# Expert rows found by one-hot products and fetched, and expert weights moved by transfers, in an attention and mixture-of-experts layer

## The chip, the cores and the metric

The kernel runs on one core of a Trainium2 chip. Times are device microseconds of one execution. The engines are TensorE (PE; PEld is its weight load), VectorE (DVE), ScalarE (ACT), GpSimd (POOL) and SyncE (SP), which here only issues transfers. Sixteen DMA engines carry all transfers, whichever queue issues them.

## What is computed

`x` is 16 x 256 x 128. After a layer norm without weights, two branches read the same `xn`:

```python
xn = _layernorm(x, axis=-1)
# attention: 16 heads of 8, causal, with a rising position bias; q, k, v have a low-rank addition
s = s + alibi[None] + mask
p = jax.nn.softmax(s, axis=-1)
o = einsum(p, v) ; s = o @ Wp.T
# experts: each token goes to the one expert of 8 with the largest logit
indices = jnp.argmax(softmax(xn @ Wr + br), axis=-1)
for i in range(num_experts):
    mask = (indices == i)[..., None]
    h = jax.nn.relu((xn * mask) @ W1[i] + b1[i])
    out = out + (h @ W2[i] + b2[i])
return x + s * silu(out)
```

The 4,096 tokens have one expert each (128 to 512 hidden to 128). For the seven other experts a token's row of `xn` is zero, so they add a constant row, worked out once.

## The kernel before, in words

**The loop.** After a prologue, every engine runs the same two loops: 16 iterations `i` (one batch of 256 tokens each), each of six groups `g` (`NG`). A group holds two units of scores (the last one): PE computes the scores of batch `i` (L1142, mask L1150) and, for the row maxima, those of batch `i + 2` (L1122, mask L1130). DVE takes the row maxima (L807), ACT the exponentials (L698), PE multiplies them with the values (L1193). Between them, at fixed groups, lie the rest of a batch's work: the turned maxima (L1204, L618), which SP writes into the stack of queries (L383); the output copied out of its bank by ACT (`keep_o`, L688), turned (L1213), divided (L921, L926), turned back (L1220) and projected (L1227); and the projection of batch `i + 4` (L1070), cut into three bf16 parts (L596, L781, L602, L498) that SP stores into the stack (L345, L351, L378). Eight stores of batch `i + 3` are issued at the start of iteration `i`, two more and the maxima in group 3. PE, DVE and ACT share banks of PSUM in a fixed turn (four for DVE, three for ACT); `VEC` and `ACTS` number the uses.

**The experts.** Logits are taken in iteration 0, the best expert, the counts per tile and each token's slot (`slot_of`, L876) at the end of iteration 0 and the start of iteration 1. Slots are sorted by expert and padded to tiles of 128, at most 39 (`SLOT_TILES`). A table of slots in DRAM (`sorted_rows`) is cleared in iteration 0 (L390, five transfers), and from iteration 1 to 6 POOL scatters one tile of normalised rows per group, with the token's number beside each row (L505, 32 of them). At the start of iteration 7, when all have landed, SP loads four tiles of sorted rows at a time (L412); POOL keeps the numbers (L512).

**A tile** `t` then is: PE turns the rows (four tiles at once, `turn_rows`, L1235) and ACT copies them (L675); ACT reads the expert's number and copies its 578 KB of weights from `w_all` into one of three slots (`copy_weights`, L682), one tile ahead; PE `hidden` (L1243), DVE relu with the bias (L933), PE `output` (L1251) one group later, DVE adds the constant row (L939), POOL scatters the result to the tokens' places (L518). One tile stands in each group, from group 43 (7, 1) on. `TILES_AT`, `TURN_AT` and the other tables map a place `(i, g)` to it. The eight expert weights are loaded in iterations 1 to 4 (L402), the constant rows computed in iteration 5 (L1263, 64 records).

**The end.** From group 84 on SP loads the experts' results (L421), ACT takes the tanh (L670), DVE multiplies (L954, L960), DVE or POOL adds x, SP stores. The last batch is finished behind the loop.

## Time and profile before

| | us |
|---|---|
| median of 3 runs | 356.69 (356.25 to 358.17) |
| the profiled execution | 357.79 |
| its span, first to last instruction | 356.0 |
| PE busy | 303.9 (85%) |
| DVE, ACT, POOL busy | 215.9, 208.0, 115.3 |
| mean granted clock of PE | 0.922 of full speed |

Busy time of an engine is the union of its instructions; matmuls are pipelined, so a busy PE need not be at its peak. Iterations are told apart in the trace by L688, ACT's copy of the output, once per iteration from iteration 1 on: 74.1, 90.1, 105.4, 118.9, 132.1, 155.3, 167.0, 198.2, 220.8, 242.9, 265.5, 287.5, 309.0, 326.3, 338.1 and 347.7 us.

### The profile page before, as it was taken

The page shows a single profiled execution, that of the slowest core. Times are in us where ns is not written, and L with a number is a line of the kernel's source. Part 1 is how long each engine was busy: PE and PEld are TensorE (multiplying, and loading weights), DVE is VectorE, ACT ScalarE, POOL GpSimd, SP SyncE. Part 2 cuts the span into 40 slices and gives each one's busy share as a digit, 9 for nine tenths or more (in the row PEclk, how much of TensorE's full clock was granted, in tenths as well). Part 3 has the DMA queues.
Part 4 walks back from the last instruction along what each step waited for, and adds up shares of the span by engine and source line. Part 5 has one row for each costly group of instructions (what it writes and reads, how often), then busy time and mean ns, then how long its engine had stood idle before and what let it go on. Part 6 is the DMA issues. An engine that isn't in the chain of part 4 may idle for free.

```text
span 356.0 us, 12916 instructions
## 1 busy us (share of the span) xinstructions
PE 303.9 (85%) x5244; PEld 234.3 (66%) x5244; DVE 215.9 (61%) x501; ACT 208.0 (58%) x380; POOL 115.3 (32%) x143
## 2 busy tenths in 40 slices
PE   6866697988778879986299999999999999999773
PEld 2445585755555557654188888888888888887542
DVE  3747893475856751674065756757567575664495
ACT  2242235256657661567177777777777776766881
POOL 5532191006355550441022242422424222222150
PEclk9966589579999999899589999999999999999997
DMA  7995340235365662142402422225222241010753
GB/s 191 225 194 126 103 160 28 113 79 176 106 203 151 179 206 54 45 111 51 125 18 60 127 70 72 59 58 133 71 67 61 63 126 42 17 31 19 215 148 115
DMA packets 47946, 37.36 MB, mean 105 GB/s; under 512 B 5016, under 2 KB 44824, under 8 KB 47760
## 3 DMA queue, kind: packets, MB, share of 16 engines
q1 hardware_dynamic: 43856, 29.73, 30.9%
q0 software_dynamic: 2272, 4.92, 4.2%
q10 hardware_dynamic: 1760, 1.89, 2.6%
q8 instruction: 42, 0.69, 0.9%
q14 instruction: 16, 0.13, 0.1%
HBM read 13.46 MB, written 9.96 MB: 66 GB/s over the span
## 4 chain that ended last, share of the span: by engine, by line
PE 70%; DVE 8%; issue 7%; DMA 6%; ACT 5%; SPq 2%; ACTq 1%; DVEq 0%
PE bank L1243 11%; PE bank L1193 10%; PE bank L1142 10%; PE bank L1251 9%; PE bank L1070 4%; PE bank L1077 3%; PE bank L1150 3%; PE bank L1227 3%; PE bank L1122 2%; PE bank L1086 2%; PE bank L1213 2%; PE bank L1263 2%; PE bank L1235 2%; DMA dense<-w_dense 2%; DVE row_max L807 1%
## 5 line engine op out<-in xcount | busy, mean ns | idle before, releaser
L807 DVE TENSOR_REDUCE row_max<-bank 128x2 f32<-128x512 f32 (+3 forms) x176 | 107.1, 638 | 53.1 <-PE bank L1130 44.0
L698 ACT ACTIVATE probs<-bank 128x512 f32<-128x512 f32 (+1 forms) x176 | 91.6, 559 | 48.5 <-PE bank L1150 41.1
L1142 PE MATMUL bank<-qk_stack 64*64 64x64 bf16 (+3 forms) x1024 | 64.7, 241 | 10.4 <-issue 3.6
L1122 PE MATMUL bank<-qk_stack 64*64 64x64 bf16 (+3 forms) x1024 | 68.6, 252 | 5.0 <-DVE row_max L807 1.8
L518 POOL DMA_INDIRECT expert_rows<-y_slot,token_of x39 | 37.7, 967 | 95.0 <-DVE y_slot L939 95.0
L1142 PEld LDWEIGHTS bank<-qk_stack 64*64 64x64 bf16 x1024 | 36.8, 110 | 28.5 <-issue 16.0
L1193 PE MATMUL bank<-probs,v_diag 128*32 128x64 f32 (+3 forms) x1024 | 50.2, 313 | 3.6 <-issue 3.3
L505 POOL DMA_INDIRECT sorted_rows<-rows_all,slot_of x32 | 31.0, 970 | 59.7 <-PE bank L1150 55.9
L682 ACT ACTIVATE w_slots<-w_all 128x1156 f32 x39 | 45.5, 1167 | 4.0 <-issue 2.7
L1130 PE MATMUL bank<-cb 64*64 64x128 bf16 (+2 forms) x352 | 46.7, 259 | 0.1
L933 DVE TENSOR_TENSOR hT<-bank,w_slots 128x512 f32<-128x512 f32 x39 | 26.9, 690 | 30.9 <-PE bank L1243 30.9
L1243 PE MATMUL bank<-xsT_slot,w_slots 128*128 128x128 f32 x312 | 44.4, 283 | 1.3 <-issue 0.8
L1150 PE MATMUL bank<-cb 64*64 64x128 bf16 (+2 forms) x352 | 45.3, 248 | 0.0
L1122 PEld LDWEIGHTS bank<-qk_stack 64*64 64x64 bf16 x1024 | 38.1, 115 | 7.7 <-DVE row_max L807 2.9
L1243 PEld LDWEIGHTS bank<-xsT_slot,w_slots 128*128 128x128 f32 x312 | 38.7, 192 | 4.3 <-issue 2.9
L1251 PE MATMUL bank<-w_slots,hT 128*128 128x128 f32 x312 | 41.2, 275 | 0.0
L1251 PEld LDWEIGHTS bank<-w_slots,hT 128*128 128x128 f32 x312 | 38.0, 192 | 0.0
L1193 PEld LDWEIGHTS bank<-probs,v_diag 128*32 128x32 f32 x1024 | 26.8, 112 | 16.7 <-issue 5.9
L498 POOL TENSOR_TENSOR parts<-rem,parts 128x512 bf16<-128x512 f32 x16 | 18.4, 1153 | 31.9 <-ACT parts L602 31.3
L1130 PEld LDWEIGHTS bank<-cb 64*64 64x64 bf16 x352 | 21.6, 117 | 0.7 <-issue 0.3
L1070 PE MATMUL bank<-xnT_all,w_eff 128*128 128x256 f32 x64 | 19.4, 435 | 2.6 <-ACT xnT_all L590 2.0
L1150 PEld LDWEIGHTS bank<-cb 64*64 64x64 bf16 x352 | 20.9, 111 | 0.7 <-issue 0.6
(122 smaller groups left out, 369.6 us busy)
## 6 DMA issues: line engine op xcount, KB each, us to landing
qk_stack<-parts SPq DMA_DIRECT2D x120, 64.0 KB
qk_stack<-parts SPq DMA_DIRECT2D x32, 128.0 KB
w_all<-w_experts SPq DMA_DIRECT2D x8, 512.0 KB
sorted_rows<-w_all SPq DMA_DIRECT2D x5, 576.0 KB, 3.9
xs_slot<-sorted_rows SPq DMA_DIRECT2D x9, 288.0 KB
rows_all<-expert_rows SPq DMA_DIRECT2D x8, 256.0 KB, 4.2
out<-rows_all SPq DMA_DIRECT2D x7, 256.0 KB, 2.3
x_all<-x SPq DMA_DIRECT2D x3, 512.0 KB, 15.0
```

The lines of the kernel that those rows point to most:

```text
L518: pool.indirect_dma_start(y_dram[:, :], bass.IndirectOffsetOnAxis(token_of[:, t:t + 1], axis=0), y_slot[:, t % 3, :], None).then_inc(S[f"y ...
L682: act.activation(w_slot[t % 3], w_all[:, bass.ds(e, 1), :].rearrange("p o f -> p (o f)"), ACT.Copy).then_inc(S["w_done"], 1)
L698: act.activation(probs[:, m % PROBS, 0:w], bank[:, 0:w], ACT.Exp).then_inc(emptied, 1)
L807: dve.tensor_reduce(row_max[b % 2][:, n, pairs[0]:pairs[-1] + 1], bank[:, 0:ln_u * len(pairs)].rearrange("p (c k) -> p c k", k=ln_u), AX.X ...
L1070: last = pe.matmul(bank[:, n * T:(n + 1) * T], w_eff[:, n, :], xnT_all[:, b, :], start=(n == 0), stop=True, skip_group_check=True)
L1122: pe.matmul(bank[to, c * ln_u:(c + 1) * ln_u], q[rows, p, n * BLK:(n + 1) * BLK], k[rows, p, 0:(n + 1) * BLK], start=(c == 0), stop=False, ...
L1130: last = pe.matmul(bank[to, 0:ln_u * len(pairs)].rearrange("p (c k) -> p c k", k=ln_u)[:, :, n * BLK:], ident_b[rows, rows], mask_qk[rows] ...
L1142: pe.matmul(bank[rows, c * ln_u:(c + 1) * ln_u], k[rows, p, kb * BLK:(kb + 1) * BLK], q[rows, p, kb * BLK:], start=(c == 0), stop=False, s ...
L1150: last = pe.matmul(bank[rows, 0:ln_u * len(pairs)].rearrange("p (c k) -> p c k", k=ln_u)[:, :, 0:BLK], ident_b[rows, rows], mask_kq[rows]. ...
L1193: last = pe.matmul(pv_bank[32 * j:32 * j + 32, half * T + kb * BLK:(half + 1) * T], v_diag[b % 2][:, kb, p, :], probs[:, (b * NU + w) % PR ...
L1243: last = pe.matmul(bank[:, c * P:(c + 1) * P], w_slot[t % 3][:, c * P:(c + 1) * P], xsT_slot[:, t // 4 % 2, t % 4, :], start=(c == 0), sto ...
L1251: last = pe.matmul(bank[:, 0:D], hT[:, t % 2, c, :], w_slot[t % 3][:, W2 + c * D:W2 + (c + 1) * D], start=(c == 0), stop=(c == NC_H - 1))
```

## The change

- **Whose row a slot holds** is found by products. DVE splits a token's slot into tile and row (`r32[:, 4]`, `r32[:, 5]`), DVE and POOL make one-hot arrays of both in iteration 1, and PE multiplies them (`slot_tokens`, 32 products at (1, 5)); DVE keeps the token numbers (`from_row`, `token_of`).
- **Rows.** SP stores the normalised rows in order (`keep_rows`, four transfers of 512 KB); POOL fetches 128 rows per tile with an indirect transfer (`fetch_rows`), eight tiles ahead. Clearing, scattering and the loads of sorted rows go.
- **Weights.** `copy_weights` issues a transfer from ACT's queue into the slot, SBUF to SBUF, with a semaphore per slot, in place of an activation.
- **Places.** Tiles start at group 17 (2, 5) in place of 43, four per iteration (groups 5, 0, 2, 3) in place of six. The constant rows move from iteration 5 to 2, the expert loads to iterations 0 and 1, the bias columns to (0, 2), the last part from group 84 to 77.

```diff
-FIRST_SCATTER = NG + 2
-FIRST_TILE = FIRST_SCATTER + NT + 3
-TURNS = list(range(FIRST_TILE, FIRST_TILE + SLOT_TILES))
+ROWS_TURN = 2 * NG + 4
+TILE_OFFSETS = (1, 2, 4, 5)
+TURNS = [ROWS_TURN + t // 4 * NG + TILE_OFFSETS[t % 4] for t in range(SLOT_TILES + 1)]
...
 TILES_AT = {place: (t,) for t, place in enumerate(PLACES)}
-SCATTER_AT = {divmod(FIRST_SCATTER + n, NG): n for n in range(NT)}
 QUADS = (SLOT_TILES + 3) // 4
-ROWS_PLACE = divmod(FIRST_TILE - 1, NG)
-TURN_AT = {PLACES[max(4 * q - 2, 0)]: q for q in range(1, QUADS)} | {ROWS_PLACE: 0}
...
-EXPERT_AT = {(1 + e // 2, 4 + e % 2): e for e in range(E)}
+ROWS_PLACE = divmod(ROWS_TURN, NG)
+TURN_AT = {PLACES[4 * q - 2]: q for q in range(1, QUADS)} | {ROWS_PLACE: 0}
+FETCH_AT = {divmod(ROWS_TURN - 3 + n, NG): (2 * n, 2 * n + 1) for n in range(4)}
+FETCH_AT |= {PLACES[t - 8]: (t,) for t in range(8, SLOT_TILES)}
+EXPERT_AT = {(0, g): g for g in range(NG)} | {(1, 1): 6, (1, 2): 7}
+KEEP_ROWS_AT = {(0, 3): 0, (0, 4): 1, (0, 5): 2, (1, 4): 3}
 K_ON_ACT = 2
-CROW_AT = (5, 1)
-CROW_SPREAD_AT = (5, 2)
+CROW_AT = (2, 2)
+CROW_SPREAD_AT = (2, 3)
...
+HOT_AT = {(1, 1): "high", (1, 2): 0, (1, 3): 1, (1, 4): "ids"}
+HOT_VEC, HOT_POOL = (0, 1), (2, 3)
+IDS_AT = (1, 5)
 
 
 CHUNK = 4
 CHUNKS = NT // CHUNK
-FIRST_LOAD = TURNS[-1] + 3
+FIRST_LOAD = TURNS[-1] + 2
...
-            def clear_rows(c):
+            def keep_rows(c):
 
                 if c == 0:
-                    sp.wait_ge(S["zero_rows_src"], 1)
-                rows = ROWS_PER_P // ZERO_CHUNKS
-                sp.dma_start(xs_dram.rearrange("(p n r) d -> p n (r d)", p=P, n=ZERO_CHUNKS)[:, c],
-                             clear_src[:, c * rows:(c + 1) * rows].rearrange("p r d -> p (r d)")).then_inc(S["zeros_out"], 16)
+                    sp.wait_ge(S["xn_vec"], len(NORM_VEC))
+                    sp.wait_ge(S["xn_act"], len(NORM_ACT))
+                sp.wait_ge(S["xn_pool"], len([n for n in NORM_POOL if n < 8 * (c + 1)]))
+                sp.dma_start(xn_tiles[:, 8 * c:8 * (c + 1), :], xn_all[:, 8 * c:8 * (c + 1), :]).then_inc(S["rows_kept"], 16)
...
-            def load_rows(q):
-                tiles = min(4, SLOT_TILES - 4 * q)
-                if q == 0:
-                    sp.wait_ge(S["scattered"], 16 * NT)
-                if q >= 2:
-                    k, use = ACTS["rows", q - 2]
-                    sp.wait_ge(act_full[k], use + 1)
-                    sp.wait_ge(S["tokens_kept"], q - 1)
-                sp.dma_start(xs_slot[:, q % 2, 0:tiles, :],
-                             xs_dram[4 * q * P:(4 * q + tiles) * P].rearrange("(j p) d -> p j d", p=P)).then_inc(S[f"xs_in{q % 2}"], 16)
...
-            def scatter(n):
-
-                pool.indirect_dma_start(xs_dram[:, :], bass.IndirectOffsetOnAxis(slot_of[:, n:n + 1], axis=0),
-                                        rows_all[:, n, :], None).then_inc(S["scattered"], 16)
-
-            def keep_tokens(q):
-
-                pool.wait_ge(S[f"xs_in{q % 2}"], 16 * (q // 2 + 1))
-                tiles = min(4, SLOT_TILES - 4 * q)
-                pool.tensor_copy(token_of[:, 4 * q:4 * q + tiles], xs_slot[:, q % 2, 0:tiles, ROW_TOKEN].bitcast(U32)).then_inc(S["tokens_kept"], 1)
+            def row_onehot(c):
+
+                for n in range(8 * c, 8 * (c + 1)):
+                    pool.tensor_scalar(row_hot[:, n, :], iota_row, r32[:, 5, n:n + 1], None, ALU.is_equal).then_inc(S["row_hot_pool"], 1)
+
+            def fetch_rows(t):
+
+                q = t // 4
+                if t == 0:
+                    pool.wait_ge(S["rows_done"], 1)
+                    pool.wait_ge(S["rows_kept"], 16 * 4)
+                if q >= 2:
+                    wait_act_full(pool, "rows", q - 2)
+                pool.indirect_dma_start(xs_slot[:, q % 2, t % 4, :], None, xn_dram[:, :],
+                                        bass.IndirectOffsetOnAxis(from_row[:, t:t + 1], axis=0)).then_inc(S[f"xs_in{t % 8}"], 16)
...
                 e = act.value_load(tile_expert[0:1, t:t + 1], min_val=0, max_val=E - 1)
                 if t >= 3:
                     wait_vec_emptied(act, "y", t - 3)
-                act.activation(w_slot[t % 3], w_all[:, bass.ds(e, 1), :].rearrange("p o f -> p (o f)"), ACT.Copy).then_inc(S["w_done"], 1)
+                act.dma_start(w_slot[t % 3], w_all[:, bass.ds(e, 1), :].rearrange("p o f -> p (o f)")).then_inc(S[f"w_in{t % 3}"], 16)
...
-                dve.tensor_copy(slot_of[:, :], r32[:, 3, :]).then_inc(S["slots_done"], 1)
+                then(dve.tensor_copy(r32i[:, 0, :], r32[:, 3, :]))
+                then(dve.tensor_scalar(r32i[:, 1, :], r32i[:, 0, :], P.bit_length() - 1, None, ALU.arith_shift_right))
+                then(dve.tensor_copy(r32[:, 4, :], r32i[:, 1, :]))
+                dve.scalar_tensor_tensor(r32[:, 5, :], r32[:, 4, :], -float(P), r32[:, 3, :], ALU.mult, ALU.add).then_inc(S["slots_done"], 1)
+
+            def tile_onehot():
+
+                hot = [P, NT, SLOT_ROWS]
+                then(dve.tensor_tensor(tile_hot[:, :, 0, :], iota_slot.unsqueeze(1).to_broadcast(hot),
+                                       r32[:, 4, :].unsqueeze(2).to_broadcast(hot), ALU.is_equal))
+
+            def tile_numbers():
+
+                then(dve.tensor_tensor(tile_hot[:, :, 1, :], tile_hot[:, :, 0, :], tile_ids.unsqueeze(2).to_broadcast([P, NT, SLOT_ROWS]), ALU.mult))
+                dve.tensor_scalar(tile_hot[:, :, 0, :], tile_hot[:, :, 0, :], place1, None, ALU.mult).then_inc(S["tile_hot_done"], 1)
+
+            def row_onehot(c):
+
+                dve.wait_ge(S["slots_done"], 1)
+                tiles = slice(8 * c, 8 * (c + 1))
+                dve.tensor_tensor(row_hot[:, tiles, :], iota_row.unsqueeze(1).to_broadcast([P, 8, P]),
+                                  r32[:, 5, tiles].unsqueeze(2).to_broadcast([P, 8, P]), ALU.is_equal).then_inc(S["row_hot_vec"], 1)
+
+            def keep_ids():
+
+                bank, emptied = wait_vec_full(dve, "ids")
+                then(dve.tensor_copy(r40[:, 0, :], bank[:, 0:SLOT_ROWS]))
+                dve.scalar_tensor_tensor(r40[:, 1, :], bank[:, SLOT_ROWS:2 * SLOT_ROWS], float(P), r40[:, 0, :], ALU.mult, ALU.add).then_inc(emptied, 1)
+                wait_vec_emptied(dve, "ids")
+                dve.tensor_scalar(from_row[:, :], r40[:, 1, :], -1.0, 0.0, ALU.add, ALU.max).then_inc(S["rows_done"], 1)
+                then(dve.scalar_tensor_tensor(r40[:, 0, :], r40[:, 1, :], 0.0, spare_ids, ALU.is_equal, ALU.mult))
+                dve.scalar_tensor_tensor(token_of[:, :], r40[:, 1, :], -1.0, r40[:, 0, :], ALU.add, ALU.add).then_inc(S["tokens_done"], 1)
...
-                    if (i, g) == (2, 1):
+                    if (i, g) == (0, 2):
+                        bias_columns()
+                    if (i, g) in HOT_AT:
+                        if HOT_AT[i, g] == "high":
+                            tile_onehot()
+                        elif HOT_AT[i, g] == "ids":
+                            tile_numbers()
+                        else:
+                            row_onehot(HOT_AT[i, g])
+                    if (i, g) == IDS_AT:
+                        keep_ids()
+                    if (i, g) == (2, 0):
...
+            def slot_tokens():
+
+
+                pe.wait_ge(S["tile_hot_done"], 1)
+                bank, full = begin_vec("ids")
+                for n in range(NT):
+                    if n // 8 in HOT_VEC:
+                        pe.wait_ge(S["row_hot_vec"], n // 8 + 1)
+                    else:
+                        pe.wait_ge(S["row_hot_pool"], n + 1 - 8 * len(HOT_VEC))
+                    last = pe.matmul(bank[:, 0:2 * SLOT_ROWS], row_hot[:, n, :], tile_hot[:, n].rearrange("p c h -> p (c h)"),
+                                     start=(n == 0), stop=(n == NT - 1))
+                last.then_inc(full, 1)
...
-                pe.wait_ge(S[f"xs_in{q % 2}"], 16 * (q // 2 + 1))
                 bank, full = begin_act("rows", q)
                 for j in range(min(4, SLOT_TILES - 4 * q)):
+                    pe.wait_ge(S[f"xs_in{(4 * q + j) % 8}"], 16 * (q // 2 + 1))
                     last = pe.transpose(bank[:, j * P:(j + 1) * P], xs_slot[:, q % 2, j, 0:D], ident_f)
                 last.then_inc(full, 1)
 
             def hidden(t):
-                pe.wait_ge(S["w_done"], t + 1)
+                pe.wait_ge(S[f"w_in{t % 3}"], 16 * (t // 3 + 1))
```

The order of PE in an iteration with tiles, before (scores and masks left out; L1193 products with the values, L1235 turn of rows, L1243 and L1251 hidden and output, L1213, L1220, L1227 the attention output, L1204 the maxima):

```order
L1235 MATMUL bank<-cf,xs_slot 128x128 x4
L1243 MATMUL bank<-xsT_slot,w_slots 128x128 x4
L1251 MATMUL bank<-w_slots,hT 128x128 x4
...
L1193 MATMUL bank<-probs,v_diag 32x256 x8
L1204 MATMUL bank<-cb,nmax 32x64 x8
L1243 MATMUL bank<-xsT_slot,w_slots 128x128 x4
L1251 MATMUL bank<-w_slots,hT 128x128 x4
...
L1220 MATMUL bank<-cf,o_tok 128x128 x2
L1077 MATMUL bank<-w_v,xnT_all 64x64 x8
L1243 MATMUL bank<-xsT_slot,w_slots 128x128 x4
```

And after, from group 1 to group 3 of an iteration (line numbers of the changed kernel: L1271 turn of rows, L1279 hidden, L1287 output):

```order
L1249 MATMUL bank<-cf,oT 128x128 x4
L1092 MATMUL bank<-xnT_all,w_eff 128x256 x2
...
L1229 MATMUL bank<-probs,v_diag 32x256 x8
L1240 MATMUL bank<-cb,nmax 32x64 x8
L1271 MATMUL bank<-cf,xs_slot 128x128 x4
L1279 MATMUL bank<-xsT_slot,w_slots 128x128 x4
L1287 MATMUL bank<-w_slots,hT 128x128 x4
...
L1256 MATMUL bank<-cf,o_tok 128x128 x2
L1099 MATMUL bank<-w_v,xnT_all 64x64 x8
L1279 MATMUL bank<-xsT_slot,w_slots 128x128 x4
```

Group 1 has no tile now; the turn of rows stands in group 2, straight ahead of a hidden product, and groups 2 and 3 keep one tile each.

ACT in groups 2 and 3, before (L698 exponentials, L602 second part, L618 maxima, L682 the copy of weights):

```order
192 L602 ACTIVATE parts<-rem 128x512 [waits q2_out3,vec_empty2]
193 L618 ACTIVATE nmaxT<-bank 64x256 [waits act_full2,max_in0]
194 L679 TENSOR_LOAD tile_expert
195 L679 ISA x2
196 L682 ISA
197 L682 ACTIVATE w_slots<-w_all 128x1156
198 L698 ACTIVATE probs<-bank 128x384 [waits act_full0,pv_ps]
```

and after (L679 exponentials, L583, L599 and L656 as L602, L618 and L675 before):

```order
120 L583 ACTIVATE parts<-rem 128x512 [waits q2_out3,vec_empty2]
121 L599 ACTIVATE nmaxT<-bank 64x256 [waits act_full2,max_in0]
122 L656 ACTIVATE xsT_slot<-bank 128x512 [waits act_full0]
123 L660 TENSOR_LOAD tile_expert
124 L660 ISA x2
125 L663 ISA [waits vec_empty2]
126 L663 DMA w_slots<-w_all 128x1156
127 L679 ACTIVATE probs<-bank 128x384 [waits act_full1,pv_ps]
```

The transfer is issued where the copy stood, one tile ahead of its use, and in group 2 the copy of turned rows stands ahead of it.

DVE in iteration 1 after the change, groups 1 to 5 (L789 row maxima, L866, L871, L872 the tile one-hots, L878 the row one-hots, L884 on the token numbers); before, only the row maxima stood there:

```order
L866 TENSOR_TENSOR w_slots<-cf,r 128x32x40
L763 TENSOR_TENSOR rem<-bank,parts 128x512
L789 TENSOR_REDUCE row_max<-bank 128x2 x2
L878 TENSOR_TENSOR w_slots<-cf,r 128x1024
L789 TENSOR_REDUCE row_max<-bank 128x2 x2
L878 TENSOR_TENSOR w_slots<-cf,r 128x1024
L789 TENSOR_REDUCE row_max<-bank 128x4 x2
L871 TENSOR_TENSOR w_slots<-w_slots,cf 128x32x40
L872 TENSOR_SCALAR w_slots<-w_slots,cf 128x32x40
L789 TENSOR_REDUCE row_max<-bank 128x8
L884 COPY r<-bank 128x40
```

Five large passes now stand between the row maxima for which PE's banks wait.

## Rows read from the trace of the kernel before

**Rows 1.** The page, busy time: us, share of the span, instructions.
```profile
PE 303.9 (85%) x5244; PEld 234.3 (66%) x5244; DVE 215.9 (61%) x501; ACT 208.0 (58%) x380; POOL 115.3 (32%) x143
```
**Rows 2.** Busy time by stretch, core 0: iterations 1, 2, 5, 6, 7, 9, 14, 15, tail.
```profile
core 0: us, PE busy (x) PEld busy (x) DVE busy (x) ACT busy (x) POOL busy (x), PEclk, DMA share, GB/s
74.10:90.10 16.00, 12.46 (x292) 8.52 (x294) 10.82 (x30) 9.40 (x20) 6.19 (x6) 0.98 0.47 140
90.10:105.40 15.30, 11.90 (x277) 7.75 (x271) 10.58 (x28) 8.94 (x19) 6.93 (x7) 1.00 0.51 156
...
132.10:155.30 23.20, 21.52 (x364) 15.11 (x357) 10.85 (x22) 9.20 (x19) 6.92 (x7) 0.93 0.22 59
155.30:167.00 11.70, 10.06 (x262) 6.94 (x253) 8.01 (x17) 8.88 (x20) 4.05 (x4) 1.00 0.32 81
167.00:198.20 31.20, 22.31 (x357) 18.54 (x358) 13.48 (x30) 16.95 (x28) 5.44 (x7) 0.84 0.27 73
...
220.80:242.90 22.10, 21.91 (x377) 18.83 (x376) 14.15 (x30) 16.47 (x26) 7.13 (x8) 1.00 0.25 68
...
326.30:338.10 11.80, 9.54 (x195) 6.58 (x190) 4.74 (x9) 9.57 (x23) 1.28 (x1) 1.00 0.58 163
338.10:347.70 9.60, 7.39 (x140) 4.47 (x136) 9.50 (x13) 7.50 (x18) 4.60 (x3) 1.00 0.56 158
347.70:356.00 8.30, 2.32 (x10) 1.55 (x10) 4.42 (x10) 0.98 (x2) 0.00 (x0) 0.72 0.35 101
```
**Rows 3.** Timeline of SP at 172, the chain of waits there, and the list of waits.
```profile
172.47 1.14 SPq L412 DMA_DIRECT2D xs_slot<-sorted_rows  x2
```
```profile
172.47 3.15 DMA xs_slot<-sorted_rows
```
```profile
PE bank L1235 <- DMA xs_slot<-sorted_rows: 8.8, 1, 8.8
```
**Rows 4.** Timeline of PE, iterations 8 and 9: start us, us, engine, line.
```profile
205.76 1.16 PE L1243 MATMUL bank<-xsT_slot,w_slots 128*128 128x128 f32 x8
206.76 1.06 PE L1251 MATMUL bank<-w_slots,hT 128*128 128x128 f32 x8
207.75 0.27 PE L1142 MATMUL bank<-qk_stack 64*64 64x192 bf16 x2
...
209.41 1.16 PE L1243 MATMUL bank<-xsT_slot,w_slots 128*128 128x128 f32 x8
...
216.49 1.06 PE L1243 MATMUL bank<-xsT_slot,w_slots 128*128 128x128 f32 x8
```
```profile
220.48 1.14 PE L1243 MATMUL bank<-xsT_slot,w_slots 128*128 128x128 f32 x8 [0.43 <-issue]
```
**Rows 5.** The chain of waits, the constant rows.
```profile
134.30 7.08 PE bank L1263 x64
```
**Rows 6.** Groups by shape: count, busy us, mean ns, idle before.
```profile
L682 ACT ACTIVATE w_slots<-w_all 128x1156 f32 x39 | 45.5, 1167 | 4.0 <-issue 2.7
L501 POOL TENSOR_SCALAR rows_all<-x_all,rstd,nmr 128x128 f32<-128x128 f32 x27 | 11.7, 450 | 12.0 <-DVE nmr L770 11.9
L807 DVE TENSOR_REDUCE row_max<-bank 128x2 f32<-128x512 f32 x64 | 42.3, 686 | 22.4 <-PE bank L1130 15.4 <-issue 2.6 <-remote 2.3
L960 DVE TENSOR_TENSOR rows_all<-rows_all,xnT_all 128x512 f32<-128x512 f32 x7 | 6.9, 992 | 0.0
L954 DVE SCALAR_TENSOR_TENSOR rows_all<-w_slots,rows_all 128x512 f32<-128x512 f32 x8 | 6.7, 836 | 5.8 <-ACT w_slots L670 5.8
L852 DVE TENSOR_TENSOR xs_slot<-xs_slot,cf 128x256 f32<-128x256 f32 x1 | 0.4, 426 | 0.0
```
**Rows 7.** L390, stores of 576 KB: issue to landing; one microsecond while three are under way.
```profile
DMA to landing us min/median/max: 2.9/3.9/6.8
```
```profile
44.00:45.00 1.00, 1.00 (x14) 0.48 (x11) 1.00 (x3) 0.00 (x0) 1.00 (x3) 0.50 1.04 424
```
**Rows 8.** Timeline of ACT's queue: a store issued beside an activation.
```profile
19.46 0.54 ACTq L351 DMA_DIRECT2D qk_stack<-parts  x1
```

101 lines of the change are left out of this document (44 added, 57 removed).

## The prediction

> **What bounds the kernel now.** The busy line of the page comes first: TensorE 85%, the others 32 to 61% [rows 1]. That is an average, so the second view is busy time by stretch, one stretch per iteration of the loop over the 16 batches (from one copy of the attention output out of the banks to the next) [rows 2]. Read PE's busy time against the stretch. With six expert tiles in an iteration (220.8 to 242.9) PE is busy 21.91 of 22.10 us: it is the bound, ACT and DVE have 5.6 and 8 us to spare. Without tiles (155.3 to 167.0) the same attention takes 11.7 us, PE busy 10.06: about 1.4 us goes into hand-overs between engines. Iterations 1 and 2 take 16.0 and 15.3. Two stretches stand out: 23.2 us, which holds the constant rows (7.08 us of PE in the chain of waits [rows 5]), and 31.2 us, the first with tiles. The third view, waits and the chain around 172, says why: the first load of sorted rows leaves SP at 172.47, behind eight stores of projections, lands after 3.15 us, and PE has waited 8.8 us [rows 3]; it then runs part of the stretch at the lower clock (granted 0.84 on average, 1.00 in its neighbours) [rows 2].
>
> So there are four places with slack: that start, the tile-free iterations where PE idles, the last two iterations (9.54 of 11.8 and 7.39 of 9.6 us busy), and the tail. PE's own work must be done whatever its order.
>
> **The change, part by part.** Times are of the profiled execution (span 356.0, its own time 357.79); I move only the difference onto the median 356.69. Everything before 74.1 I leave as it is: expert loads take the place of the zero stores in the same queue, and three copies of normalised rows (512 KB each) are added there behind a queue whose next stores go out at 71. From 74.1 to the end is 281.9 us before. The same part after, iteration by iteration:
>
> 1. Iterations 3 to 11, four tiles each. A tile costs PE 1.99 us here (205.76 to 207.75, hidden and output products) and somewhat under where it doesn't follow a small product; I take 1.9 [rows 4]. Attention, six tiles and one turn of rows are 22.1; less 2 x 1.9 is 18.3. Two of six groups now have no tile to cover hand-overs; a tile-free iteration loses 1.4 over all six, of which I put 0.3 here. 18.6 x 9 = 167.4.
> 2. Iteration 12: two hidden and three output products left, 22.1 - 3.5 x 1.9 = 15.4.
> 3. Iteration 1. VectorE gets two compares of 1,024 elements per partition, three passes of 1,280 and about nine small ones. 256 elements take 0.426 and 512 take 0.686 us [rows 6], so 1,024 cost 1.2, 1,280 cost 1.5, a small one 0.2 (estimates): 2.4 + 4.4 + 1.6 = 8.4 us. VectorE is busy 10.82 of 16.0, so 5.2 hide and 3.2 do not. PE then runs 32 products; nothing like them is in the trace, the 64 of the constant rows take 0.11 each, so at most 3.5 us, at least nothing exposed, and I take 1.3 beyond what VectorE's backlog covers. GpSimd makes 16 one-hots at 0.45 = 7.2 us [rows 6] where scatters were; it finishes before PE's last group. 16.0 + 4.5 = 20.5.
> 4. Iteration 2 takes in the constant rows: 23.2 - 11.7 = 11.5 with its hand-overs, 10.5 where the stretch is looser anyway; one turn of rows and one hidden product, 1.5; the scatters and expert loads that made it longer than 11.7 are gone, -2.0. 15.3 + 10.5 + 1.5 - 2.0 = 25.3.
> 5. Iterations 13 to 15 and the tail. The gates now start two groups into iteration 13, where VectorE still has its 11 row maxima (8 us busy in a tile-free iteration); four products at 0.84 and three at 0.99 [rows 6] bring it to 14.3, so 14.5. Iteration 14 goes from 11.8 to 10.3 (PE 9.54 plus hand-overs; nothing waits for the last scatter any more), 15 from 9.6 to 8.5 (PE 7.39; VectorE, busy 9.50 of 9.6 before, has only the last gates), the tail from 8.3 to 7.5, since the last division no longer queues behind gates. 40.8.
>
> Sum 167.4 + 15.4 + 20.5 + 25.3 + 40.8 = 269.4 against 281.9: **-12.5 us** if every weight transfer is hidden. The start of the tiles is in it: the rows are fetched by GpSimd two to three groups ahead and no longer queue on SP.
>
> 6. The weights. ACT's copy is 1.17 us, 39 times [rows 6], but ACT doesn't bound, so taking it away is worth nothing by itself; an issue takes ACT's queue 0.54 us beside the activation that runs [rows 8]. What counts is the time from issue to landing, since tile t+1's transfer is issued in tile t's group and PE waits for it. The nearest row is a store of 576 KB with 128 runs of 4.6 KB, against 578 KB here in the same runs: 2.9 us at least, 3.9 median (several of them queued behind one another), 6.8 at most, at 424 GB/s in the full microsecond [rows 7]. The time that PE gives it: hidden product to hidden product in neighbouring groups is 3.65 us (205.76 to 209.41) and 3.99 (216.49 to 220.48) [rows 4]; the issue comes about 0.5 after the first of them (the read of the expert's number, and in every other case the copy of turned rows ahead of it). That leaves 3.15 and 3.5. Nineteen of the 38 gaps are of that kind, the others span two groups and have 2 us more. Alone the transfer fits by 0.2 to 0.6 us. But 39 x 578 KB is 23 MB, four transfers an iteration at 1.5 us of all 16 engines = 6 us, beside the 0.25 of the engines' time in use now in an iteration with tiles [rows 2], which comes in bursts. I take 0.3 us of wait on each of the nineteen: **+6 us**. Ends: 0 (2.9 always) and 19 x 1.2 = +23 (4.4 us, the median plus half a microsecond).
>
> The Trainium skill ("DMA: Bandwidth & Descriptors", section "Anatomy of one DMA") gives a fixed cost of about 2.0 us plus bytes over 436 GB/s for a transfer: by our arithmetic 3.4 us here, 0.5 over the 2.9 of the row. By it alone the 3.15 us gaps would wait 0.2 each and the longer ones not at all, some 2 us in all; the row's minimum would give none.
>
> -12.5 + 6 = -6.5: 356.7 - 6.5 = **350.2 us**.
>
> **Rivals.** (A) *The transfers land late*, and that is the one that ends slower. Mechanism: ACT's transfers meet the eight stores of projections and the row maxima's transfer; at 4.4 us to landing the nineteen waits cost 1.2 each and the sum is -12.5 + 23 = +10.5, 367 us. It decides from 0.66 us per wait on (12.5 / 19), that is from landings of some 4.0 us, hardly over the median of the row. For it: the second issue of ACT slips when ACT is behind; the transfer reads and writes SBUF, which the row doesn't. Against: DMA is in use for a quarter of an iteration with tiles now [rows 2], and SP's stores go out 0.6 us apart, so a large transfer gets most of the engines. The skill (same page, "Issuing engines are not separate DMA queues") says that transfers interleave on the same engines whoever issues them; the row on which this bears is the most loaded one, 6.8 us.
>
> (B) *All hidden*: -12.5, 344 us. For it, the minimum of 2.9 and the two-group gaps; a wait also lets ACT and VectorE catch up for the tile-free group behind it.
>
> (C) *The order costs more than it gives*: iteration 1 bound by VectorE at 24 instead of 20.5 and a low clock after PE's idling, iterations 3 to 11 at 19.0 instead of 18.6: +3.5 +3.6 = 357, no change.
>
> That the change doesn't do what it says would be that ACT's issues hold its exponentials up as long as the copies did; at 0.54 against 1.17 and with ACT at three quarters busy this changes nothing.
>
> **How the numbers follow.** Forecast (347 to 354.5): 0.38. B (under 347): 0.24. C (355 to 358.5): 0.12. A (over 358.5): 0.26. The range 340 to 366 leaves out the ends of A and B, about 0.15 to 0.2. Faster by over 0.5% (about what a measurement of this kernel can tell from no change), under 354.9: 0.62; within 0.5%: 0.12; slower: 0.26.
>
> **What would show it.** Right: no wait of 8 us before the first turn of rows; iterations 3 to 11 at 18.6 to 19.2 us, PE busy over 95%; landings of the weights at 3.0 to 3.7 us and PE's waits on them under 0.6 us each, nineteen or fewer; iteration 1 at 20 to 21 us with VectorE over 90% busy; iteration 14 near 10. Wrong: iterations at 20 us or more with the hidden product waiting on the transfer (A), or waits elsewhere in iterations 1, 2 and 13 (C). If the load on the DMA engines delays the projections' stores, the first scores of an iteration would wait for them; that would be a mechanism that I have priced at nothing, because the last of them and the row maxima go out in group 3, some 8 us before PE needs them.

## Result and profile after

| | median, us | range | runs |
|---|---|---|---|
| before | 357.43 | 356.25 to 359.91 | 4 |
| changed | 378.51 | 377.01 to 379.74 | 4 |

The ratio is 1.0578, with a 95% interval of 1.0507 to 1.065: 5 to 6.5% slower. The forecast was 350.2, with a range that ended at 366. Some executions of a kernel come out more than 1.5% above its fastest; the ratios, and the medians marked with a star below, leave them out.

The page of the changed kernel, its head and the groups that answer to [rows 1] and [rows 6]; of a group: busy time, mean duration of one, and the idle time of the engine just before them with what ended it.

```profile
span 375.1 us, 12978 instructions
PE 305.3 (81%) x5276; PEld 236.1 (63%) x5276; DVE 220.0 (59%) x514; ACT 162.4 (43%) x341; POOL 128.8 (34%) x152
...
q10 hardware_dynamic: 7376, 24.97, 18.7%
...
DMA w_slots<-w_all 19%; PE bank L1279 8%; PE bank L1287 6%; PE bank L1178 5%; PE bank L1229 4%; PE bank L1186 3%; ACT probs L679 3%; PE bank L1249 2%; PE bank L1092 2%; PE bank L1299 2%; PE bank L1263 1%; DVE rem L763 1%; DMA xn_all<-expert
...
L1279 PE MATMUL bank<-xsT_slot,w_slots 128*128 128x128 f32 x312 | 49.2, 300 | 33.4 <-DMA w_slots<-w_all 25.2
```

TensorE is still the busiest engine, but at 81% instead of 85%, and the chain that ended last now holds a transfer for a fifth of the span: `w_slots<-w_all`, the experts' weights. It is the new entry, and PE waited 25.2 us for it ahead of the hidden products (L1279). The weights are 23 of the 25 MB on q10, ACT's queue.

The same stretches as in [rows 2], one per iteration (PE, PEld, DVE, ACT, POOL busy, then the granted clock of PE, the DMA engines' share and GB/s): iterations 1 to 5, then 10 to 15 and the tail.

```profile
71.40:93.20 21.80, 14.59 (x315) 10.24 (x317) 18.18 (x44) 9.10 (x19) 15.07 (x17) 0.89 0.47 132
93.20:121.20 28.00, 23.09 (x359) 16.87 (x356) 12.15 (x26) 9.52 (x20) 10.87 (x11) 0.88 0.31 94
121.20:143.00 21.80, 19.20 (x350) 15.70 (x349) 12.42 (x26) 9.76 (x21) 9.04 (x9) 1.00 0.50 164
143.00:165.30 22.30, 18.94 (x345) 15.26 (x344) 12.42 (x26) 9.36 (x21) 9.03 (x9) 1.00 0.51 169
165.30:189.10 23.80, 19.12 (x345) 15.36 (x344) 12.47 (x26) 9.38 (x21) 9.03 (x9) 1.00 0.52 168
...
281.00:300.20 19.20, 17.54 (x339) 14.32 (x338) 12.54 (x26) 9.56 (x21) 6.08 (x6) 1.00 0.56 179
300.20:322.50 22.30, 19.61 (x341) 16.40 (x341) 12.42 (x26) 9.34 (x20) 5.03 (x5) 0.92 0.48 159
322.50:337.50 15.00, 14.36 (x318) 11.32 (x322) 9.55 (x20) 7.95 (x18) 2.88 (x3) 1.00 0.37 108
337.50:349.00 11.50, 9.90 (x270) 6.72 (x262) 11.16 (x23) 9.88 (x24) 2.55 (x2) 1.00 0.71 205
349.00:360.10 11.10, 8.87 (x184) 6.18 (x182) 10.00 (x18) 9.10 (x22) 2.59 (x2) 1.00 0.43 123
360.10:368.10 8.00, 7.49 (x146) 4.68 (x142) 0.78 (x2) 5.65 (x13) 0.00 (x0) 1.00 0.14 37
368.10:375.10 7.00, 1.80 (x10) 1.14 (x10) 2.39 (x6) 0.98 (x2) 0.00 (x0) 0.86 0.13 37
```

Iterations 3 to 11 run from 121.2 to 322.5 and take 201.3 us, 22.4 each, where 18.6 was forecast. PE is busy 17.5 to 20.2 of each, so it no longer fills them. The first load of rows, for which PE waited 8.8 us in [rows 3], has no such wait any more: that part of the change works.

What PE waited for in those nine iterations (us in total, times, longest):

```profile
PE bank L1279 <- DMA w_slots<-w_all: 19.6, 16, 3.4
PE bank L1279 <- issue: 8.0, 10, 2.5
```

Sixteen waits at 19.6 / 16 = 1.2 us. Eleven of them, 14.6 us, stand on gaps of one group between two tiles, and five, 5.0 us, on gaps over two groups, to which the prediction gave no wait. Besides, "issue": PE stood still and the profile shows nothing that it waited for. Three of these ten (1.6, 1.9 and 2.5 us, just ahead of a hidden product) may well be weights too; the other seven are 0.2 to 0.5 us long, and such stops come back below.

A wait on a gap of one group, ACT's queue and then PE; the hidden product of the tile before starts at 286.65:

```profile
287.49 0.51 ACTq L663 DMA_DIRECT2D w_slots<-w_all  x1
...
291.06 1.16 PE L1279 MATMUL bank<-xsT_slot,w_slots 128*128 128x128 f32 x8 [0.78 <-DMA w_slots<-w_all]
```

The issue comes 0.84 us after the product before it and the weights land 3.6 us later: 4.4 together, where PE gets there in 3.6.

A wait on a gap over two groups. The hidden product of the tile before starts at 175.36:

```profile
176.94 0.49 ACT L679 ACTIVATE probs<-bank 128x384 f32<-128x384 f32 x1 [2.41 <-remote]
177.32 0.38 ACT L640 ACTIVATE o2T<-bank 128x256 f32<-128x256 f32 x1
177.59 0.37 ACT L590 ACTIVATE v_diag<-bank 64x256 f32<-64x256 f32 x1
177.87 0.50 ACTq L663 DMA_DIRECT2D w_slots<-w_all  x1
...
183.19 1.05 PE L1279 MATMUL bank<-xsT_slot,w_slots 128*128 128x128 f32 x7 [2.26 <-DMA w_slots<-w_all]
```

The transfer is issued 2.5 us after the hidden product before it, behind an exponential and two copies in ACT's queue ("remote": released by a queue that the profile doesn't name), and lands 5.3 us later. The prediction had 0.5 and 2.9 to 3.9.

### The profile page after: what moved, and what is told of

It is laid out like the page before. It is cut to its first block, busy times and chain, and to the rows that moved or that the text cites. A ratio compares the mean times of both kernels' runs of the same rounds, so it can differ in the third digit from the quotient of the medians.

```text
span 375.1 us, 12978 instructions
## 1 busy us (share of the span) xinstructions
PE 305.3 (81%) x5276; PEld 236.1 (63%) x5276; DVE 220.0 (59%) x514; ACT 162.4 (43%) x341; POOL 128.8 (34%) x152
## 3 DMA queue, kind: packets, MB, share of 16 engines
q10 hardware_dynamic: 7376, 24.97, 18.7%
## 4 chain that ended last, share of the span: by engine, by line
PE 37%; DMA 21%; ACT 6%; issue 5%; DVE 4%; another core or an unknown queue 2%; ACTq 1%; POOL 0%; DVEq 0%; SPq 0%
DMA w_slots<-w_all 19%; PE bank L1279 8%; PE bank L1287 6%; PE bank L1178 5%; PE bank L1229 4%; PE bank L1186 3%; ACT probs L679 3%; PE bank L1249 2%; PE bank L1092 2%; PE bank L1299 2%; PE bank L1263 1%; DVE rem L763 1%; DMA xn_all<-expert_rows 1%; ACTq L660 1%
## 5 line engine op out<-in xcount | busy, mean ns | idle before, releaser
L679 ACT ACTIVATE probs<-bank 128x512 f32<-128x512 f32 (+1 forms) x176 | 91.9, 559 | 123.7 <-PE bank L1186 98.1
L789 DVE TENSOR_REDUCE row_max<-bank 128x2 f32<-128x512 f32 (+3 forms) x176 | 107.8, 637 | 41.4 <-PE bank L1166 24.6
L1279 PE MATMUL bank<-xsT_slot,w_slots 128*128 128x128 f32 x312 | 49.2, 300 | 33.4 <-DMA w_slots<-w_all 25.2
L1158 PE MATMUL bank<-qk_stack 64*64 64x64 bf16 (+3 forms) x1024 | 67.2, 252 | 4.6 <-DVE row_max L789 1.8
L1178 PE MATMUL bank<-qk_stack 64*64 64x64 bf16 (+3 forms) x1024 | 63.2, 241 | 6.4 <-ACT xnT_all L571 1.8
L1279 PEld LDWEIGHTS bank<-xsT_slot,w_slots 128*128 128x128 f32 x312 | 41.1, 202 | 40.1 <-DMA w_slots<-w_all 28.9
L1178 PEld LDWEIGHTS bank<-qk_stack 64*64 64x64 bf16 x1024 | 35.7, 109 | 23.7 <-issue 11.6
L498 POOL DMA_INDIRECT xs_slot<-normalised_rows,from_row x39 | 38.0, 974 | 33.0 <-PE bank L1186 26.1
L1229 PE MATMUL bank<-probs,v_diag 128*32 128x64 f32 (+3 forms) x1024 | 47.3, 314 | 0.2 <-ACT probs L679 0.2
L1166 PE MATMUL bank<-cb 64*64 64x128 bf16 (+2 forms) x352 | 46.2, 259 | 0.0
L1186 PE MATMUL bank<-cb 64*64 64x128 bf16 (+2 forms) x352 | 44.4, 247 | 0.0
L1287 PE MATMUL bank<-w_slots,hT 128*128 128x128 f32 x312 | 43.4, 284 | 0.0
L1158 PEld LDWEIGHTS bank<-qk_stack 64*64 64x64 bf16 x1024 | 37.8, 115 | 7.7 <-DVE row_max L789 2.9
L1287 PEld LDWEIGHTS bank<-w_slots,hT 128*128 128x128 f32 x312 | 40.2, 201 | 0.1
L480 POOL TENSOR_TENSOR parts<-rem,parts 128x512 bf16<-128x512 f32 x16 | 18.5, 1155 | 47.1 <-ACT parts L583 47.1
L488 POOL TENSOR_SCALAR w_slots<-cf,r 128x128 bf16<-128x128 f32 x16 | 14.0, 891 | 19.7 <-DVE r L861 19.7
L1092 PE MATMUL bank<-xnT_all,w_eff 128*128 128x256 f32 x64 | 18.5, 420 | 2.4 <-ACT xnT_all L571 2.0
```

The costliest lines, as they stand in the source:

```text
L498: pool.indirect_dma_start(xs_slot[:, q % 2, t % 4, :], None, xn_dram[:, :], bass.IndirectOffsetOnAxis(from_row[:, t:t + 1], axis=0)).then_ ...
L679: act.activation(probs[:, m % PROBS, 0:w], bank[:, 0:w], ACT.Exp).then_inc(emptied, 1)
L789: dve.tensor_reduce(row_max[b % 2][:, n, pairs[0]:pairs[-1] + 1], bank[:, 0:ln_u * len(pairs)].rearrange("p (c k) -> p c k", k=ln_u), AX.X ...
L1158: pe.matmul(bank[to, c * ln_u:(c + 1) * ln_u], q[rows, p, n * BLK:(n + 1) * BLK], k[rows, p, 0:(n + 1) * BLK], start=(c == 0), stop=False, ...
L1166: last = pe.matmul(bank[to, 0:ln_u * len(pairs)].rearrange("p (c k) -> p c k", k=ln_u)[:, :, n * BLK:], ident_b[rows, rows], mask_qk[rows] ...
L1178: pe.matmul(bank[rows, c * ln_u:(c + 1) * ln_u], k[rows, p, kb * BLK:(kb + 1) * BLK], q[rows, p, kb * BLK:], start=(c == 0), stop=False, s ...
```

## The experiments

Each kernel ran beside the kernel before on the same chip, and kernels of one group on one chip. The five groups ran on five chips, and this turned out to matter: the kernel before took 357.07, 357.2 and 357.74 us on three of them (as in the result above), and 344.12 and 343.68 us on the other two. Below, a **357 chip** and a **344 chip**. No chip was met twice, so that the chip makes the difference, and not something else that differed from group to group, is inferred and not shown. Line numbers are the changed kernel's, and shift by one or more in kernels with added or removed lines. Where code is shortened, "..." marks it.

### The weights' transfers

**e1_copy**, a 357 chip: the changed kernel, with the one part undone.

```diff
-act.dma_start(w_slot[t % 3], w_all[:, bass.ds(e, 1), :]...).then_inc(S[f"w_in{t % 3}"], 16)
+act.activation(w_slot[t % 3], w_all[:, bass.ds(e, 1), :]..., ACT.Copy).then_inc(S["w_done"], 1)
```

> The changed kernel with one part undone: the weights are again copied into their slot by ScalarE (1.17 us each) instead of by a transfer; rows, one-hot products and places stay as changed. Theory L (the loss is PE waiting for weights that have not landed): the 31 us of waits named for the weights go, part of the gain is given back to waits elsewhere, 345 to 352 us. Theory D (the load of 23 MB on the DMA engines slows other things, whoever waits for it): the same kernel is fast as well, 345 to 352, since the load is gone; the run with an unused load tells these apart. Theory P (the new places and the routing cost more than they give): it stays above 365 us.

Measured: 357.0 us (353.87 to 359.59, 10 runs), ratio to before 1.0009 (0.9966 to 1.0052). All of the loss goes with the transfers; but the 12.5 us that the rest of the change should give are not there either.

**e2_before_xfer**, the same chip: the kernel before, with this one part of the change done.

```diff
-act.activation(w_slot[t % 3], w_all[...], ACT.Copy).then_inc(S["w_done"], 1)
+act.dma_start(w_slot[t % 3], w_all[...]).then_inc(S[f"w_in{t % 3}"], 16)
```

> The kernel before with one part done alone: weights come by transfers from ScalarE's queue, everything else as before. All 38 gaps between tiles are one group here. Theory L: each waits for about 1 to 1.5 us more, 395 to 410 us. Theory D: less, since no more load arrives per microsecond than in the changed kernel, 370 to 385. Theory P: no change, 357.

Measured: 385.75 us (383.5 to 391.24), ratio 1.0767 (1.0687 to 1.0846): +28.7, in the other order of the work too. PE's wait there:

```profile
PE bank L1243 <- DMA w_slots<-w_all: 22.0, 23, 2.2
```

**e3_two_ahead**, the same chip: the changed kernel with a fourth weight slot, each transfer issued two tiles ahead.

```diff
-w_slots = sb("w_slots", [P, 3, WB])
+w_slots = sb("w_slots", [P, 4, WB])
...
-if t + 1 < SLOT_TILES:
-    copy_weights(t + 1)
+if t + 2 < SLOT_TILES:
+    copy_weights(t + 2)
```

The weights of tiles 0 and 1 are both issued ahead of the first tile.

> The changed kernel with four weight slots in place of three, and each transfer issued two tiles ahead in place of one (three small arrays share the place of others to make room). The load on the DMA engines is the same, the time until the weights are needed about 6 us longer. Theory L: no waits for weights, 345 to 353 us. Theory D: the waits for weights go but half of the loss stays, 360 to 370. Theory P: 365 and more.

Measured: 358.05 us (355.47 to 364.98, 10 runs), ratio 1.0013 (0.9971 to 1.0055). The same 23 MB go over the same engines, and by the medians 1 us is left of the loss. So it is the time to landing against a lead of one tile that costs, and hardly the load.

**e4_copy_load**, the same chip: e1_copy, with an unused transfer of the same size on ACT's queue for each tile.

```diff
+if t > 0:
+    act.wait_ge(S["load0"], 16 * t)
+act.dma_start(spare[:, :], w_all[:, bass.ds(e, 1), :]...).then_inc(S["load0"], 16)
```

ACT also waits here for the unused transfer of the tile before, which can only make the kernel slower.

> The weights copied by ScalarE as in the run with copies, and beside each copy an unused transfer of the same 578 KB from the same place into a spare array, issued by ScalarE's queue, which nothing on PE or VectorE waits for. Theory L: within 3 us of the run with copies. Theory D: 8 to 20 us above it, with gaps on PE that no compute instruction ends.

Measured: 360.05 us (355.69 to 361.69, 10 runs), ratio 1.0062 (1.0013 to 1.0111). By the medians the load, with that wait, costs 3 us; the interval overlaps that of e1_copy, so 0 to some 5.

**f1_after** (a 357 chip, beside f2_copy) and **g1_after** (a 344 chip, beside g2_copy): the changed kernel once more, to see the price of the transfers on one chip.

> The changed kernel once more, beside the three that follow. The kernel before took 357.07 us beside e1_copy to e4_copy_load, and 344.12 beside e5_no_fetch to e8_burst_fetch, so two chips differ by 13 us in the same kernel, and what was read from one chip may not hold on the other. Theory W (the late landing of the weights costs the 21 us wherever it runs): f1_after is 19 to 24 us over f2_copy, 376 to 381 where the kernel before takes 357 and 354 to 360 where it takes 344. Rival (the landing is late only on the slower chip): where the kernel before takes 344, f1_after is within 8 us of f2_copy.

> The changed kernel, beside g2_copy on the same chip. Theory W (the landing costs 19 to 25 us on any chip): 19 to 26 us over g2_copy, 376 to 381 where the kernel before takes 357, 353 to 360 where it takes 344. Rival (late only on a chip on which the kernel before takes 357): within 8 us of g2_copy where it takes 344.

Measured: f1_after 380.67 us (373.99 to 384.89), g1_after 369.6 us (363.65 to 372.23), four runs each. f1_after is 21.9 us over f2_copy (375.7* and 353.8*) and g1_after 32.5 over g2_copy (366.0* and 333.6*; the starred medians of f1_after and g1_after rest on two runs each). The transfers cost on both kinds of chip, and more than the 19 to 26 expected where everything else is faster. Iterations 3 to 9 of g2_copy and of g1_after, and PE's wait in the latter:

```profile
116.60:243.20 126.60, 126.26 (x2397) 104.76 (x2398) 85.66 (x182) 99.65 (x169) 62.09 (x62) 1.00 0.30 77
```
```profile
117.80:270.30 152.50, 131.47 (x2390) 107.92 (x2388) 86.10 (x183) 66.75 (x141) 62.54 (x63) 0.97 0.55 173
...
PE bank L1279 <- DMA w_slots<-w_all: 19.7, 16, 2.8
```

Of the 25.9 us between the two stretches 19.7 are waits for the weights, and 5.2 are longer busy time of PE for the same products: the granted clock is 0.97 instead of 1.00. Three of the seven iterations of g1_after were granted 0.92 or 0.93, with PE busy 19.7 or 19.8 us; the other four were granted 1.00, with 17.7 to 18.2. g2_copy, which doesn't wait, was granted 1.00 all through. So the waits slow PE a second time, by the clock.

### The gain that was missing

In e1_copy, iterations 3 to 9 take 20.7 us each and 10 and 11 take 18.7 and 18.4 (18.6 was forecast for all). What ends between them is the row fetches of GpSimd, whose last is for tile 38 in iteration 10. PE's waits in iterations 3 to 9 of e1_copy:

```profile
PE bank L1279 <- issue: 6.7, 18, 0.6
PE bank L1099 <- issue: 3.0, 6, 0.5
```

PE stops for about half a microsecond, some three to four times an iteration, with nothing shown that it waits for.

**e5_no_fetch**: e1_copy without the fetches from tile 8 on; the later tiles are computed on the rows of the first eight.

```diff
-FETCH_AT |= {PLACES[t - 8]: (t,) for t in range(8, SLOT_TILES)}
```

> e1_copy without the indirect fetches of tiles 8 to 38: these tiles are computed on the rows that tiles 0 to 7 left in their slots, so the fetching of 31 tiles' rows is left out, and everything else stays. In e1_copy iterations 3 to 9 took 20.4 to 21.0 us each and iterations 10 and 11, in which one fetch and none are left, 18.7 and 18.4. Theory F (the fetches, issued by GpSimd beside the expert products, cost TensorE about 2 us an iteration): iterations 3 to 9 fall to 18.4 to 18.8, the time from 357.0 to 342 to 344. Theory G (the fetches are innocent, and iterations 10 and 11 are short for another reason, such as the q and k stores that end there): iterations 3 to 9 stay at 20.4 to 21.0 and the time at 356 to 358.

**e6_plain_fetch**: rows of tiles 8 to 38 by SyncE, 128 neighbouring rows and not those that the tile asks for.

```diff
-FETCH_AT |= {PLACES[t - 8]: (t,) for t in range(8, SLOT_TILES)}
+PLAIN_AT = {PLACES[t - 8]: (t,) for t in range(8, SLOT_TILES)}
...
+for t in PLAIN_AT.get((i, g), ()):
+    q = t // 4
+    wait_act_full(sp, "rows", q - 2)
+    wait_act_full(sp, "scores", i, GROUPS[g][0])
+    sp.dma_start(xs_slot[:, q % 2, t % 4, :], xn_dram[P * (t % 16):P * (t % 16 + 1), :]).then_inc(S[f"xp_in{t % 8}"], 16)
```

> e1_copy with the rows of tiles 8 to 38 brought by a plain transfer of SyncE at the same places: 128 rows of 512 bytes that lie next to each other in DRAM, and not the rows that the tile's slots ask for, so the computation of the routing is left out there. If what costs is GpSimd's indirect DMA itself (its descriptors, its issuing), iterations 3 to 9 are 18.4 to 18.8 us as expected of e5_no_fetch by theory F, and the time 342 to 345. If what costs is the traffic of 64 KB from DRAM beside the stores, they stay at 20.4 to 21.0, and the time at 355 to 358. By theory G nothing changes either, and e5_no_fetch tells the two apart.

**e7_hot_vec**: one-hots of 24 instead of 16 tiles on VectorE.

```diff
-HOT_VEC, HOT_POOL = (0, 1), (2, 3)
+HOT_VEC, HOT_POOL = (0, 1, 2), (3,)
...
+if (i, g) == (1, 3):
+    row_onehot(2)
```

> e1_copy with 24 instead of 16 tiles' row one-hots on VectorE (three operations over 8 tiles) and 8 instead of 16 on GpSimd. In the changed kernel GpSimd took 0.89 us for each of 16, 14.0 us in all, and TensorE waited for them in iteration 1 of 21.8 us (20.7 in e1_copy). Theory H (GpSimd's second half ends last): iteration 1 is 1 to 3 us shorter, the time 354 to 356. Rival (VectorE is as full there, its row maxima come later by the 1.2 us of the added operation): iteration 1 stays within 0.7 us of 20.7, the time within 1 us of 357.0.

**e8_burst_fetch**: four fetches behind one another.

```diff
-FETCH_AT |= {PLACES[t - 8]: (t,) for t in range(8, SLOT_TILES)}
+FETCH_AT |= {PLACES[4 * q - 8]: tuple(range(4 * q, min(4 * q + 4, SLOT_TILES))) for q in range(2, QUADS)}
```

> e1_copy with the same 31 fetches, but the four of a quad issued one behind the other at the place of its first tile, instead of one in each of four groups. Theory F says that each fetch costs TensorE something where it is issued. If the price belongs to each fetch, about 0.5 us, iterations 3 to 9 stay at 20.4 to 21.0 us and the time at 355 to 358. If it comes from a fetch that meets the expert products and the stores, the groups with no fetch are cheaper, and the time is 345 to 353. If four in a row keep the y scatter behind them on GpSimd (1 us each) and y's slots come free late, it is 358 to 364.

Measured, all four on a 344 chip (before 344.12):

| | median, us | ratio to before | iterations 3 to 9, each |
|---|---|---|---|
| e5_no_fetch | 334.75 | 0.9741 (0.9685 to 0.9796) | 18.1 |
| e6_plain_fetch | 334.46 | 0.9747 (0.9677 to 0.9816) | 18.1 |
| e7_hot_vec | 336.63 | 0.9773 (0.969 to 0.9856) | 18.1 |
| e8_burst_fetch | 333.47 | 0.9674 (0.9599 to 0.9749) | 18.0 |

Read against e1_copy, e5_no_fetch alone would have "shown" that the fetches cost 22 us. Read within its group it shows the opposite: with the fetches (e7_hot_vec), without them, in ones or fours, the iterations are the same. The chip is another one, and there the fetches have no price that shows. So nothing about the fetches follows for a 357 chip, and the four had to be run again beside a copy kernel. Of e7_hot_vec: its iteration 1 was 22.8 us, against 20.1 to 21.5 in e5_no_fetch, e6_plain_fetch, e8_burst_fetch and g2_copy; a third compare on VectorE helps nothing.

**f2_copy**, **f3_no_fetch** and **f4_burst** are e1_copy, e5_no_fetch and e8_burst_fetch on one chip, which was a 357 chip.

> e1_copy once more. Theory C (the missing gain is the chip's: the chip that is slower for the kernel before slows the changed order by more): where the kernel before takes 344, iterations 3 to 11 are 18.0 to 18.6 us each and the time is 332 to 337; where it takes 357, they are 20.4 to 21.0 in 3 to 9, and the time 355 to 359. Rival (iterations 3 to 9 of 20.6 belong to e1_copy's placing of the fetches on any chip): 344 or more even where the kernel before takes 344.

> e5_no_fetch once more, to be compared with f2_copy on the same chip; the fetching of 31 tiles' rows is left out. Theory F, that the fetches cost TensorE 2 us an iteration: 12 to 15 us below f2_copy. By theory C: on a chip where the kernel before takes 344, within 2 us of f2_copy, iterations of 18.1; on one where it takes 357 this run tells whether the fetches are what that chip is slow at (342 to 345) or not (355 to 359).

> e8_burst_fetch once more, to be compared with f2_copy on the same chip. By theory C within 2 us of f2_copy on a chip where the kernel before takes 344. On one where it takes 357: with f3_no_fetch faster than f2_copy, 345 to 353 if groups without a fetch are then cheaper, 355 to 358 if each fetch has its price; with f3_no_fetch as slow as f2_copy, 355 to 359.

| before 357.2 | median, us | ratio to before | iterations 3 to 9, each |
|---|---|---|---|
| f2_copy | 354.11 | 0.9902 (0.9845 to 0.9959) | 20.7 |
| f3_no_fetch | 340.41 | 0.9529 (0.9472 to 0.9586) | 18.5 |
| f4_burst | 383.21 | 1.0665 (1.0553 to 1.0777) | 24.3 |

On this 357 chip the fetches cost 13.7 us, and four behind one another 29.1 us more. The stretch of iterations 3 to 9 with its waits, f2_copy:

```profile
118.70:263.40 144.70, 132.20 (x2398) 106.77 (x2397) 86.21 (x182) 99.14 (x169) 63.17 (x63) 1.00 0.27 70
...
PE bank L1279 <- issue: 6.6, 18, 0.6
PE bank L1099 <- issue: 3.5, 7, 0.5
```

f3_no_fetch:

```profile
119.60:249.30 129.70, 128.11 (x2397) 105.54 (x2398) 87.54 (x185) 99.07 (x169) 35.12 (x35) 1.00 0.24 64
PE bank L1278 <- issue: 1.2, 7, 0.2
```

f4_burst:

```profile
121.20:291.00 169.80, 147.24 (x2396) 117.93 (x2397) 87.31 (x183) 99.31 (x168) 61.32 (x62) 0.92 0.23 59
PE bank L1229 <- issue: 22.1, 31, 1.3
```

POOL's busy time tells the fetches (35 us without them, 61 to 63 with), and beside them PE's "issue" grows from 1.2 to 10 and 22 us. The stops are not the whole price: in f4_burst PE is also busy 19.1 us longer than in f3_no_fetch for the same products, at a granted clock of 0.92 instead of 1.00. g2_copy, the same kernel as f2_copy on a 344 chip, has no wait of PE at all in that stretch: 126.26 of 126.60 us busy. One burst of f4_burst, POOL and then PE:

```profile
214.19 0.94 POOL L498 DMA_INDIRECT xs_slot<-normalised_rows,from_row  x1 [0.30 <-issue]
215.44 0.99 POOL L506 DMA_INDIRECT expert_rows<-y_slot,token_of  x1 [0.30 <-issue]
...
215.03 0.22 PE L1229 MATMUL bank<-probs,v_diag 128*32 128x64 f32 x1 [0.73 <-issue]
...
215.74 0.22 PE L1229 MATMUL bank<-probs,v_diag 128*32 128x64 f32 x1 [0.50 <-issue]
...
216.50 0.23 PE L1229 MATMUL bank<-probs,v_diag 128*32 128x64 f32 x1 [0.54 <-issue]
...
217.20 0.22 PE L1229 MATMUL bank<-probs,v_diag 128*32 128x64 f32 x1 [0.47 <-issue]
```

PE gets one small product out every 0.7 us. In e8_burst_fetch, beside the same four fetches on a 344 chip, 32 products of this line, of twice the length, took 0.87 us together.

### Do the fetches cost only where they meet SyncE's stores?

In f4_burst the stalls fell on the stretch in which SP also sends eight stores of projections and one of zero rows. **g3_copy_quiet** and **g4_ahead_quiet** move the fetches out of those groups, two each in groups 1 and 4; the second has e3_two_ahead's transfers. **g2_copy** is e1_copy beside them.

```diff
-FETCH_AT |= {PLACES[t - 8]: (t,) for t in range(8, SLOT_TILES)}
+FETCH_AT |= {(q + 1, g): tuple(t for t in (4 * q + g // 2, 4 * q + g // 2 + 1) if t < SLOT_TILES) for q in range(2, QUADS) for g in (1, 4)}
```

> The changed kernel with ScalarE's copies in place of the transfers. 353 to 358 where the kernel before takes 357; 332 to 336 where it takes 344, with iterations 3 to 11 of 18.1 us.

> g2_copy with the row fetches of tiles 8 to 38 moved out of the groups in which SyncE stores the q and k parts (groups 5, 0, 2 and 3) into groups 1 and 4, two in each. Theory M (a fetch costs TensorE something where it meets SyncE's stores, as four in a row did in f4_burst, whose single matmuls came 0.7 us apart beside both): iterations 3 to 9 fall from 20.6 to 18.4 to 19.3, and the time from 354 to 357 to 341 to 347, where the kernel before takes 357. Rival (each fetch costs its half microsecond anywhere): iterations 3 to 9 stay at 20.2 to 21.5, the time at 353 to 360. Where the kernel before takes 344 both expect 332 to 336, no difference.

> The changed kernel with the weights' transfers issued two tiles ahead into four slots, as in e3_two_ahead, and the fetches moved as in g3_copy_quiet. Theory M with transfers that are hidden: within 3 us of g3_copy_quiet, 341 to 348 where the kernel before takes 357. Rival (the weights' transfers crowd the DMA engines as the stores do, so that the fetches meet traffic wherever they are): iterations 3 to 9 of 20.5 to 21.5 us as in e3_two_ahead, 354 to 360.

The group fell on a 344 chip (before 343.68), where the question can't be told: g2_copy 333.94 us, ratio 0.9782 (0.9686 to 0.9878); g3_copy_quiet 336.26, 0.9846 (0.9755 to 0.9937); g4_ahead_quiet 338.31, 0.9867 (0.9781 to 0.9953). Iterations 3 to 9 are 18.1 us in all three, so the differences lie elsewhere or in the spread of runs (330.11 to 340.28 in g3_copy_quiet). The last shows once more that transfers issued two tiles ahead are hidden: PE waits for weights once, 3.3 us, for tile 0.

**h1_copy_quiet** and **h2_ahead_quiet** are the last two again, and fell on a 357 chip (before 357.74).

> g3_copy_quiet once more, for a chip on which the kernel before takes 357. Theory M (a fetch costs where it meets SyncE's stores): iterations 3 to 9 of 18.4 to 19.3 us, 341 to 347. Rival (each fetch costs its half microsecond anywhere): 20.2 to 21.5 us, 353 to 360. On a chip where the kernel before takes 344: 331 to 337 by both.

> g4_ahead_quiet once more, for a chip on which the kernel before takes 357. Theory M with hidden transfers: within 3 us of h1_copy_quiet. Rival (the weights' transfers are traffic as the stores are): iterations 3 to 9 of 20.5 to 21.5 us, 354 to 360. On a chip where the kernel before takes 344: 333 to 339 by both, as g4_ahead_quiet.

Measured: h1_copy_quiet 380.55 us, ratio 1.0677 (1.0586 to 1.0768); h2_ahead_quiet 386.78, 1.0823 (1.0751 to 1.0895). Iterations 3 to 9 take 23.7 and 24.0 us. Both of my theories fell: away from the stores the fetches cost not less but two and a half times as much (f2_copy, with 2.1 us an iteration, was on another 357 chip). h2_ahead_quiet is 6.2 us over h1_copy_quiet; 3.6 of these lie in iteration 2, where PE waits 3.1 us for the weights of tile 0. Two fetches in h1_copy_quiet, with PE's rows beside them; SP's queue issued nothing between 199.1 and 208.5:

```profile
204.12 0.97 POOL L498 DMA_INDIRECT xs_slot<-normalised_rows,from_row  x1 [0.30 <-issue]
...
205.40 0.96 POOL L498 DMA_INDIRECT xs_slot<-normalised_rows,from_row  x1 [0.30 <-issue]
205.60 0.21 PE L1158 MATMUL bank<-qk_stack 64*64 64x64 bf16 x1 [0.46 <-issue]
...
206.32 0.19 PE L1158 MATMUL bank<-qk_stack 64*64 64x64 bf16 x1 [0.48 <-issue]
...
207.05 0.21 PE L1178 MATMUL bank<-qk_stack 64*64 64x64 bf16 x1 [0.47 <-issue]
```

By the length of an iteration over f3_no_fetch's 18.5, divided by its four fetches: in ones (f2_copy) 2.1 / 4 = 0.54 us; in twos (h1_copy_quiet) 5.2 / 4 = 1.3; in fours (f4_burst) 5.7 / 4 = 1.4. But "in ones" hides something: GpSimd scatters a result per tile with an indirect transfer too, and in f2_copy three of an iteration's four fetches start 1.3 us before or after such a scatter. Only the fourth is alone. The lone one, then a scatter and a fetch, then PE beside these two:

```profile
195.89 0.97 POOL L498 DMA_INDIRECT xs_slot<-normalised_rows,from_row  x1 [1.27 <-PE bank L1186]
198.20 1.00 POOL L506 DMA_INDIRECT expert_rows<-y_slot,token_of  x1 [1.35 <-PE bank L1186]
199.51 0.97 POOL L498 DMA_INDIRECT xs_slot<-normalised_rows,from_row  x1 [0.30 <-issue]
...
200.55 0.36 PE L1279 MATMUL bank<-xsT_slot,w_slots 128*128 128x128 f32 x1 [0.55 <-issue]
201.27 0.50 PE L1279 MATMUL bank<-xsT_slot,w_slots 128*128 128x128 f32 x3 [0.37 <-issue]
```

The time from one hidden product to another tells what each costs (median of seven iterations, us; lone scatters, which all three kernels have, left out):

| from group to group | indirect transfers there in f2_copy | g2_copy | f3_no_fetch | f2_copy |
|---|---|---|---|---|
| 2 to 5 | fetch, scatter, fetch | 8.34 | 8.34 | 9.33 |
| 5 to 0 | the lone fetch | 3.45 | 3.45 | 3.46 |
| 0 to 2 | scatter (begun just ahead), fetch | 6.27 | 6.68 | 7.88 |

The lone fetch costs nothing (one of its seven gaps was 3.99), and nearly all of the price lies with the fetches that have another indirect transfer directly beside them. In h1_copy_quiet each pair stands directly behind a scatter, and in f4_burst four fetches stand ahead of one. What fits the three on a 357 chip is that indirect transfers of GpSimd directly behind one another, fetches or scatters, are the dear ones. It is not the whole rule: in the trace of before single scatters of rows (at 111.15, 124.64 and 161.04) have a stop of 0.44 to 0.48 us behind them too. Which products PE runs beside the transfers changes from place to place, and no run tells that apart.

**What stays open.** Why a 357 chip has this price and a 344 chip doesn't, and what of PE's supply is held up. That instruction blocks come late is not what the traces show: the instruction queue (q8) moved 43 packets, 0.70 MB, in either kind of run, and in f4_burst none lay between 210 and 219, around the stalls at 214 to 218. The Trainium skill ("Runtime: NRT & Kernel Launch", section "Instruction fetch mechanics") has instructions fetched in 16 KiB blocks, mostly hidden; 0.70 MB over 43 agrees with the size, and nothing here contradicts the hiding. Nor was a plain fetch tried on a 357 chip: e6_plain_fetch met the other kind, so that GpSimd's indirect form is to blame, rather than any read of these rows, isn't shown.

## Why the prediction was wrong

**Two steps failed**: step 6, which charged the weights' transfers 0.3 us on each of nineteen gaps, +6 in all, where they cost 22 us on a 357 chip; and step 1, which charged GpSimd's row fetches nothing, where they cost 13.7.

**The base sum (steps 1 to 5).** Without the transfers the change gave 9.6 of the 12.5 us on a 344 chip (g2_copy 333.6*, before 343.1*) and 0 to 3 on a 357 chip, for which the sum was made. us:

| | forecast | changed | e1_copy, 357 chip | g2_copy, 344 chip |
|---|---|---|---|---|
| iteration 1 | 20.5 | 21.8 | 20.7 | 20.1 |
| iteration 2 | 25.3 | 28.0 | 26.1 | 25.2 |
| 3 to 11 | 167.4 | 201.3 | 182.2 | 162.7 |
| 12 | 15.4 | 15.0 | 13.9 | 14.0 |
| 13 to 15 and tail | 40.8 | 37.6 | 37.9 | 37.9 |

The stretch ahead of iteration 1 is not in the sum; it ended at 71.4 instead of 74.1 us, and between 68.7 and 74.1 in the other kernels. Step 1 failed by a term that it didn't have: it took two tiles off, added for hand-overs and priced the row fetches at nothing. On a 357 chip they cost 13.7 us (f2_copy against f3_no_fetch), more than the whole -12.5. The sign was in the trace of before, in a view that I read only for its largest entry. PE's waits of before from 74 to 290 us, next to the 8.8 us of [rows 3]:

```profile
PE bank L1142 <- issue: 3.4, 8, 0.5
PE bank L1193 <- issue: 3.3, 7, 0.6
```

Of the 23 stops of this kind, twenty lie before 166, where GpSimd scattered rows (the last at 161.04), and three behind 176 (197.90, 220.48 and 265.22), where it scattered results alone. I had taken fewer scatters as a gain in step 4, without asking what the new fetches, spread over iterations 3 to 10, would cost in return.

**Iteration 1 (step 3).** 21.8 for 20.5. VectorE was busy 18.18 of it, as forecast (10.8 + 8.4 = 19.2 with some to spare; nine small passes at 0.2 would be 1.8, not the 1.6 in that sum). GpSimd's 16 one-hots took 0.60 us as a median and up to 1.95, not 0.45, 14.0 us in all, not 7.2. PE waited 0.7 us for them and 2.6 for VectorE's last pass (L872). The same iteration took 20.1 to 22.8 us in the other kernels, so 20.5 was a fair value.

**Iteration 2 (step 4).** 28.0 for 25.3. PE waited 4.3 us for the first tile's weights, to which no term was given: the transfer of tile 0 has no tile ahead of it that gives it time. With a copy in its place PE waited 2.3 us there (e1_copy), so the transfer makes about 2 of it.

**Iterations 12 to the tail.** 15.0 for 15.4, and 37.6 for 40.8: iteration 13 took 11.5, not 14.5. VectorE is busy 11.16 of it, so it is the bound as forecast, but with less to do than 14.3: three of its gates took 0.68 us each, not 0.99, and without projections to cut there is less beside them than the 8 us taken over.

**The weights (step 6).** This is the larger miss: +6 forecast, and +22 on a 357 chip (changed against e1_copy, f1_after against f2_copy), +32 on a 344 chip. The mechanism was named, and rival A had its price nearly right: 1.2 us a wait (19.6 / 16 measured) and +23. What was mis-sized is the landing against the time that PE gives it. Ahead of the sixteen waits the transfer took 3.1 to 6.5 us from issue to landing, 3.9 as a median; over all transfers of g1_after the median was 4.5, and 3.6 and 3.8 where they were issued two tiles ahead (e3_two_ahead, g4_ahead_quiet). The nearest row [rows 7] had a median of 3.9 "several of them queued", and I worked from its minimum of 2.9 for a lone transfer. And the gap was no fixed 3.15 or 3.5: the issue stands in ACT's queue behind exponentials and copies, and ahead of the sixteen waits it came 0.0 to 2.5 us after the hidden product, 0.8 as a median, not 0.5. Such slips also brought the five waits on gaps over two groups, 5.0 us, which had been taken as free. The fit of the Trainium skill that the prediction cites ("DMA: Bandwidth & Descriptors", section "Anatomy of one DMA"; 3.4 us by our arithmetic) is given there for GpSimd's path; for ACT's transfers it is short of all of these medians.

**Rivals.** A was the outcome in mechanism and in size, but its time, 367, lay on a base that was 10 to 13 us too low on such a chip (f2_copy and e1_copy against 344.2). With its decision point at 0.66 us a wait, "hardly over the median of the row", it deserved the larger chance. B fell. C's "no change" came true for a kernel without the transfers on a 357 chip (e1_copy), but by the fetches, not by VectorE or the clock.

**What would show it.** Of the signs named ahead, that of A was there (hidden products that wait on the transfer, iterations over 20 us). The stores' delay, priced at nothing, stayed at that: no wait of PE on `qk_stack<-parts` shows in iterations 3 to 11.

The kernel to keep is the changed one with the weights copied by ScalarE: 0.9902 (0.9845 to 0.9959) and 1.0009 (0.9966 to 1.0052) of before on two 357 chips, so at best 1% faster there, and 0.9782 (0.9686 to 0.9878) on a 344 chip.

## What to carry to other kernels

A transfer in place of a copy by an engine that has time to spare has to be issued ahead by its landing time under load plus whatever its issuing queue may slip. So price it with the median or worse of a row taken under load, and issue it two tiles ahead with one more buffer (e3_two_ahead), or leave the copy. Read the small entries of the bound engine's waits too: many stops of half a microsecond with no releaser, beside a kind of operation that the change adds, are a price. And compare only kernels that ran on the same chip: here two chips differ by 13 us in one kernel, and four fetches in a row cost nothing on the one and 29 us on the other.

## What the runs showed of the hardware

- One kernel took 357 us on three chips and 344 on two, each group within 0.7 us by its median. On the first kind TensorE stops for about half a microsecond at a time, with nothing shown that it waits for, beside GpSimd's indirect transfers of 128 rows of 512 bytes where these follow one another after 1.3 us. Seven iterations with 28 fetches took 15.0 us more than without; a fetch with no other indirect transfer directly beside it added 0.01 us there (3.46 against 3.45, medians of seven), though single scatters in the kernel before stopped PE for 0.44 to 0.48 us. On the second kind PE was busy 126.26 of 126.60 us with the same fetches.
- Moving the fetches away from SyncE's stores into pairs made the kernel slower on a 357 chip: the ratio to before is 1.0677 in h1_copy_quiet, and 0.9902 in f2_copy, which was on another chip of that kind.
- A transfer of 578 KB from SBUF to SBUF landed after 3.6 to 4.5 us (medians of three kernels), with 0.55 to 0.63 of the DMA engines' time in use.
- Waits of PE of 0.5 to 2.8 us, some two an iteration, came with 5.2 us more of busy time over seven iterations, at a granted clock of 0.97 instead of 1.00 (g1_after against g2_copy).
